# A decoder layer on one core: cross-attention's probabilities turned in two 64-row tiles, its values summed by 64 keys, register reads moved, all engines reordered

## The reference

```
scores = einsum('bhqd,bhkd->bhqk', qh, kh) * DH ** -0.5
scores = where((j <= i) & (j >= i - 32), scores, -1e30)
out = einsum('bhqk,bhkd->bhqd', softmax(scores), vh)  ->  out @ wo.T
```

## Time and profile before

| | |
|---|---|
| median of 3 runs | 791.24 us (790.92 to 792.99) |
| the profiled execution | 793.52 us |
| its span | 790.7 us, mean granted clock 0.987 |
| busy share of the span: PE, PEld | 96%, 80% |
| DVE, ACT, POOL | 68%, 68%, 68% |
| chain that ended last | PE 91%, DVE 3%, issue 2% |

### The profile page before, as it was taken

One profiled execution on the slowest core, in us unless ns is written; L12 is line 12 of the kernel. 1 busy time (PEld: TensorE's weight loads), 2 busy tenths in 40 slices (PEclk: granted clock), 3 DMA queues, 4 the chain that ended last, 5 costly groups with the idle time before them and its releaser, 6 DMA issues.

```text
span 790.7 us, 28613 instructions
## 1 busy us (share of the span) xinstructions
PE 759.4 (96%) x10349; PEld 631.8 (80%) x10349; DVE 536.6 (68%) x1350; ACT 539.2 (68%) x1900; POOL 535.4 (68%) x864
## 2 busy tenths in 40 slices
PE   7999999999999999999999999999899999999894
PEld 4778878888888888888888888888679778777563
DVE  3466767777777777777777777777866686665553
ACT  1367767777777777777777777777667667666352
POOL 3366777777777777777777777777565666576434
PEclk8999999999999999999999999999999999999998
DMA  6013212222222222222222222223043132133130
GB/s 232 12 56 124 80 61 82 88 91 93 92 93 73 73 73 73 72 73 73 73 73 73 73 73 72 73 73 128 9 129 125 48 101 72 40 104 123 55 101 12
DMA packets 56791, 64.06 MB, mean 81 GB/s; under 512 B 4014, under 2 KB 52916, under 8 KB 56656
## 3 DMA queue, kind: packets, MB, share of 16 engines
q1 hardware_dynamic: 52928, 54.06, 20.9%
q0 software_dynamic: 3008, 6.57, 2.4%
q10 hardware_dynamic: 720, 1.63, 0.5%
HBM read 17.80 MB, written 45.35 MB: 80 GB/s over the span
## 4 chain that ended last, share of the span: by engine, by line
PE 91%; DVE 3%; issue 2%; DMA 1%; ACT 1%; POOL 1%; SPq 0%; POOLq 0%; DVEq 0%; ACTq 0%
PE P L327 8%; PE P L272 8%; PE P L307 7%; PE P L292 7%; PE P L316 7%; PE P L338 7%; PE P L282 7%; PE P L397 5%; PE P L224 4%; PE P L207 4%; PE P L356 4%; PE P L239 4%; PE P L247 2%; PE P L364 2%; PE P L410 1%
## 5 line engine op out<-in xcount | busy, mean ns | idle before, releaser
L799 ACT ACTIVATE PX<-P,mx 128x128 f32<-128x128 f32 x512 | 182.1, 394 | 61.0 <-DVE mx L569 61.0
L966 POOL TENSOR_TENSOR PX<-PX,mx 128x512 f32<-128x512 f32 x128 | 133.0, 1041 | 62.0 <-DVE mx L574 62.0
L569 DVE TENSOR_REDUCE mx<-P 128x4 f32<-128x512 f32 x128 | 82.0, 679 | 119.3 <-PE P L307 119.3
L799 ACT ACTIVATION_READ_ACCUMULATOR PX<-P,mx 128x1 f32 x512 | 119.9, 234 | 0.0
L763 ACT ACTIVATE PS<-P 128x512 f32<-128x512 f32 x128 | 66.1, 602 | 32.0 <-PE P L228 32.0
L999 POOL DMA_INDIRECT out<-yst,xrow x46 | 46.0, 1000 | 54.6 <-DVE yst L673 42.5
L508 DVE TENSOR_REDUCE nmf<-P 128x4 f32<-128x512 f32 x128 | 79.5, 683 | 5.1 <-PE P L207 2.2
L961 POOL TENSOR_TENSOR rq<-rq,tq 128x1024 f32<-128x1024 f32 x32 | 75.7, 2365 | 8.8 <-DVE tq L533 7.8
L808 ACT ACTIVATE PT<-P 128x512 f32<-128x512 f32 x128 | 77.7, 607 | 3.5 <-PE P L316 0.8
L956 POOL TENSOR_TENSOR rk<-rk,tk 128x1024 f32<-128x1024 f32 x32 | 75.5, 2359 | 0.0
L272 PE MATMUL P<-wvT,cxT 128*128 128x512 f32 x128 | 70.4, 633 | 3.0 <-DVE tk L533 3.0
(11 more groups left out here) (144 smaller groups left out, 1757.4 us busy)
## 6 DMA issues: line engine op xcount, KB each, us to landing
z_xs<-c SPq DMA_DIRECT2D x34, 1088.0 KB, 5.3
xrow<-z_xs SPq DMA_DIRECT2D x46, 136.0 KB, 2.1
ew<-in_ew SPq DMA_DIRECT2D x9, 384.0 KB, 6.4
x<-in_x SPq DMA_DIRECT2D x32, 64.0 KB, 1.8
cxT<-in_ctxT SPq DMA_DIRECT2D x31, 64.0 KB, 1.7
out<-yst,xrow POOLq DMA_INDIRECT x46, 2.3
wk<-in_wk SPq DMA_DIRECT2D x1, 512.0 KB, 4.4
wvT<-in_wvT SPq DMA_DIRECT2D x1, 512.0 KB, 7.0
```

The lines of the kernel that those rows point to most:

```text
L569: dve.tensor_reduce(mx[b % 3][:, 0, r, :], v3(bank(f"ds{r}")), AX.X, ALU.max, negate=True).then_inc(S["v_dm"][r], 1)
L799: t = act.activation(PX[(4 * b + r) % 6][:, c, :], p[:, c * 128:c * 128 + 128], ACT.Exp, bias=m[:, 0, r, c:c + 1], scale=1.0, accum_out=m[ ...
L966: pool.tensor_tensor(X[:, :, :], X[:, :, :], mx[b % 3][:, 2, r, :].rearrange("p (h a) -> p h a", a=1).to_broadcast([128, 4, 128]), ALU.mul ...
```

## The change

1. `d_t` handles half k (8 heads) in one call. A transpose takes 64 query rows of PX instead of 128, so it has 64 columns of identity to stream and uses 64 of the array's rows; the two row halves u go to two PSUM banks. There are 32 transposes a batch for 16.
2. `PT` becomes 3 buffers of 8 heads for 6 of 4. `d_pt` still makes 4 copies of 512 elements a batch, now into columns 64u to 64u+64 of each head.
3. `d_pv` runs in tiles of 64 rows x 64 columns: `lo` multiplies keys 0 to 63 by queries 0 to 95 (96 columns), `hi` keys 64 to 127 by queries 64 to 127 (64 columns), into two banks. 32 matmuls a batch for 16.
4. ACT `d_ox` makes two copies (128 and 384 elements) for one of 512, and a new DVE `d_ox` adds `hi` to `lo` for queries 64 to 95 (128 elements); `d_wo` waits for DVE's.
5. The register read of tile j+1 stands behind `x_up(j)`'s matmul (`place`), no longer in `x_tr`.
6. The lists of all five engines, `BANK` and `WARM` are new. Cut short:

```diff
-            def d_t(b, r):
-                p = take(f"dt{r}", b, (S["s_pt"][r], b + 1))
-                pe.wait_ge(S["p_pn"][r], b + 1)
-                for c in range(4):
-                    t = pe.transpose(p[:, c * 128:c * 128 + 128], PX[(4 * b + r) % 6][:, c, :], ident[:, :])
-                t.then_inc(S["t_dt"][r], 1)
+            def d_t(b, k):
+                p = [take(f"dt{2 * k + u}", b, (S["s_pt"][2 * k + u], b + 1)) for u in range(2)]
+                for g in range(2):
+                    r = 2 * k + g
+                    pe.wait_ge(S["p_pn"][r], b + 1)
+                    for c in range(4):
+                        for u in range(2):
+                            t = pe.transpose(p[u][:, 256 * g + 64 * c:256 * g + 64 * c + 64],
+                                             PX[(4 * b + r) % 6][64 * u:64 * u + 64, c, :],
+                                             ident[64 * u:64 * u + 64, 64 * u:64 * u + 64])
+                t.then_inc(S["t_dt"][k], 1)
             def d_pv(b, k):
-                p = take(f"dpv{k}", b, (S["s_ox"][k], b + 1))
+                lo = take(f"lo{k}", b, (S["s_ox"][k], b + 1))
+                hi = take(f"hi{k}", b, (S["v_ox"][k], b + 1))
                 pe.wait_ge(S[f"s_v{k}"], b + 1)
-                for r in (2 * k, 2 * k + 1):
-                    pe.wait_ge(S["s_pt"][r], b + 1)
-                    for i in range(2):
-                        for u in range(2):
-                            q = 2 * (r % 2) + i
-                            t = pe.matmul(p[64 * u:64 * u + 64, 128 * q:128 * q + 128], V[b % 3][:, 4 * r + 2 * i + u, :],
-                                          PT[(4 * b + r) % 6][:, 2 * i + u, :], start=True, stop=True)
+                for u in range(2):
+                    pe.wait_ge(S["s_pt"][2 * k + u], b + 1)
+                for q in range(4):
+                    for u in range(2):
+                        pe.matmul(lo[64 * u:64 * u + 64, 96 * q:96 * q + 96], V[b % 3][0:64, 8 * k + 2 * q + u, :],
+                                  PT[(2 * b + k) % 3][0:64, 2 * q + u, 0:96], start=True, stop=True)
+                    for u in range(2):
+                        t = pe.matmul(hi[64 * u:64 * u + 64, 64 * q:64 * q + 64], V[b % 3][64:128, 8 * k + 2 * q + u, :],
+                                      PT[(2 * b + k) % 3][64:128, 2 * q + u, 64:128], start=True, stop=True)
                 t.then_inc(S["t_pv"][k], 1)
@@ x_up, after its matmul
+                if j + 1 < NT and j + 1 not in TILE0:
+                    place(j + 1)
@@ DVE
+            def d_ox(b, k):
+                o, hi = oX[2 * (b % 2) + k][:, :, 64:96], bank(f"hi{k}")[:, 0:256]
+                dve.wait_ge(S["s_ox"][k], b + 1)
+                dve.tensor_tensor(o, hi.rearrange("p (h q) -> p h q", h=4)[:, :, 0:32], o, ALU.add).then_inc(S["v_ox"][k], 1)
@@ ACT d_ox
-                act.activation(oX[2 * (b % 2) + k][:, :, :].rearrange("p h q -> p (h q)"), bank(f"dpv{k}"),
+                lo, hi = bank(f"lo{k}")[:, 0:384], bank(f"hi{k}")[:, 0:256]
+                act.activation(oX[2 * (b % 2) + k][:, :, 96:128], hi.rearrange("p (h q) -> p h q", h=4)[:, :, 32:64],
+                               ACT.Copy)
+                act.activation(oX[2 * (b % 2) + k][:, :, 0:96], lo.rearrange("p (h q) -> p h q", h=4),
                                ACT.Copy).then_inc(S["s_ox"][k], 1)
```

More of the change, by code:

```diff
@@ L415, in _ @@
             for s in range(PERIODS):
[L416 to L456, removed]
@@ L457, in _ @@
-                batch(b_ln, s - 5)
-                batch(d_t, s - 6, 1)
-                batch(d_t, s - 6, 2)
+                batch(b_s, s - 3)
+                tile(x_up, s - 31, 0)
+                tile(x_dn, s - 32, 1)
+                tile(x_hT, s - 32, 3)
+                batch(c_v, s - 3, 1)
+                batch(b_ln, s - 4)
+                tile(x_dn, s - 32, 2)
+                tile(x_tr, s - 31, 2)
+                batch(d_pv, s - 5, 0)
+                batch(r_q, s - 4, 0)
+                batch(e_tr, s - 6)
@@ new lines, in _ @@
+                batch(r_q, s - 4, 1)
+                batch(d_t, s - 5, 1)
+                batch(b_nm, s - 3)
+                tile(x_dn, s - 32, 3)
+                batch(f_pos, s - 7)
+                batch(f_up, s - 6)
+                batch(d_pv, s - 5, 1)
+                batch(b_st, s - 3)
+                batch(d_s, s - 4)
+                tile(x_hT, s - 31, 0)
+                tile(x_tr, s - 31, 3)
+                tile(x_up, s - 31, 1)
+                batch(b_pv, s - 3)
+                batch(d_wo, s - 5)
@@ new lines, in _ @@
+                batch(b_oT, s - 3)
+                tile(x_dn, s - 31, 0)
+                tile(x_up, s - 31, 2)
+                batch(r_k, s - 2, 0)
+                batch(a_qkv, s - 2)
+                batch(b_cn, s - 3)
+                batch(f_dn, s - 6)
+                tile(x_tr, s - 30, 0)
+                tile(x_hT, s - 31, 1)
+                batch(c_v, s - 2, 0)
+                batch(b_x1, s - 3)
+                batch(a_tr, s - 1)
+                tile(x_up, s - 31, 3)
+                tile(x_tr, s - 30, 1)
@@ L460, in _ @@
+                tile(x_hT, s - 31, 2)
+                batch(r_k, s - 2, 1)
+                batch(d_t, s - 4, 0)
             for j in range(TILE0[1], NT + 4):
@@ L676, in _ @@
             for s in range(PERIODS):
[L677 to L688, removed]
@@ new lines, in _ @@
+                batch(r_q1, s - 5)
+                batch(r_q3, s - 5)
+                batch(f_pos, s - 8)
+                tile(x_y, s - 33, 3)
+                batch(f_route, s - 7)
+                batch(f_gate, s - 7)
+                batch(d_ox, s - 6, 1)
+                batch(d_max, s - 5, 1)
+                batch(a_stats, s - 1)
+                batch(d_max, s - 5, 3)
+                batch(d_max, s - 5, 0)
+                batch(d_ri, s - 5, 1)
+                batch(d_max, s - 5, 2)
@@ L890, in _ @@
+                tile(x_xT, s - 32, 0)
+                tile(x_hT, s - 33, 1)
+                tile(x_th, s - 33, 3)
+                tile(x_hT, s - 33, 2)
+                tile(x_xT, s - 32, 1)
+                batch(c_v, s - 4, 0)
+                batch(a_norm, s - 2)
+                batch(d_pt, s - 6, 1)
+                batch(d_pt, s - 6, 0)
+                batch(b_ln, s - 5)
+                tile(x_th, s - 32, 0)
+                batch(e_norm, s - 7)
                 tile(x_hT, s - 33, 3)
+                batch(b_cT, s - 5)
```

160 lines of the change are left out of this document (75 added, 85 removed).

## The result

| | median | range (runs) |
|---|---|---|
| before, beside it | 792.12 us | 790.92 to 800.3 (4) |
| changed | **824.36 us** | 820.7 to 830.44 (4) |
| ratio | 1.0392 | 95% interval 1.0293 to 1.0491 |

The change costs 32 us; I had forecast 18 us less than before and a range up to 789. The profiled execution took 820.7 us.

The account below looks back on a forecast made before the run. PE was taken to bound the kernel, only its own time counting. 793.5 - 21.8 (turns) + 3.5 (`b_pv` wait) - 3.5 (reads) + 2.8 (end) + 1.0 (shape change in tile turns) = 775.5 us profiled, median 773, range 763 to 789.

Parts of the forecast that it names:

- `d_t`, `d_pv`: PE's transposes and value matmuls: smaller tiles run side by side, -0.80 and -0.43 us a batch.
- rivals B and C: B: weight loads bound `d_pv`'s four-tile groups, 787 us, chance 0.07. C: its row halves don't overlap, 801 us, 0.09.
- Changes of shape: PE's switches of tile shape: 11 a turn for 7, at 0.14 us each, +0.55 us a turn (0.4 to 0.75).
- The new wait at `b_pv`: PE waits in front of `b_pv` for ACT's exponentials: +0.13 us (0 to 0.25) in 27 turns, +3.5 us.
- rival A: The new order's waits take half the gain, two places missing by 0.15 us: 9.6 us back, 783 us, chance 0.20.
- the sum of a turn itself: A turn, one batch on PE: -0.80 - 0.43 + 0.55 = -0.68 us, from 20.30 to 19.6 to 19.75; 32 turns, -21.8 us.
- In such a stretch only PE's own time counts: From 200 to 240 us PE is busy all 40.00 us; the other engines have a quarter to spare.
- a floor of 25 ns: The skill's minimum between PE matmul starts, by which `d_pv` gains 0.14 instead of 0.43 us; set aside for L228's 14 ns.
- `hi1`'s bank: `d_s` takes over this bank after DVE's add: 1.98 us needed, PE there after 2.03; no cost, or 0.1 to 0.3 a turn.
- Register reads: PE's reads moved from in front of `x_tr` to behind `x_up`, mostly covered there: -3.5 us (-5 to -1).
- The end: From batch 31's `f_pos` to chunk 1's first tile: 3.4 us of PE work moves ahead, scatter 0.6 sooner, +2.8 us.

Follow-up runs that it names:

- order alone: Computation of the kernel before, in the changed kernel's new order, with the register reads moved: 824.7 us (ratio 1.0384), on another chip 855.4 us (1.0771).
- `d_pv` undone: Changed kernel with the old `d_pv`, ACT's one copy of 512 elements and no DVE add: 848.7 us, ratio 1.0697 to the kernel before.

## Why the prediction was wrong, by its own steps

- **`d_t`, `d_pv`: right.** Forecast 0.58 to 0.63 (0.48 and the shape) and 0.75 to 0.85 us a block; measured 0.64 and 0.81. Pairs and fours do run side by side; rivals B and C didn't happen.
- **Changes of shape: too small.** 11 x 0.14 less the old 7 came to +0.55. The rows behind the new blocks say more: L292 1.09 for 0.89, L216 0.16 for 0.06, L348 1.98 for 1.89, L239 1.08 for 1.01, 0.46 us. My sum was -0.68 in all with some -0.81 in the four blocks, which left 0.13 for this.
- **The new wait at `b_pv`: right place, half its size.** ACT's four exponentials took 297.57 to 299.63, and `b_pv` started 0.37 us later, where I had 0.1. From `b_st`'s end to `b_pv` it is 2.47 us, for 2.17 of `d_s` before: +0.30, not +0.13. The row of after calls this "issue"; ACT's end at 299.63 and the order alone's row speak for ACT. Together with the point above a turn is 20.2 and not 19.7: 32 x 0.5 = 16 us. The wait's part of that, 0.17 us a turn or 5 us, is rival A, which I gave 9.6 us.
- **The failed step is the sum of a turn itself, which knew columns, shapes and data and no instructions.** "In such a stretch only PE's own time counts" was read from a list with slack in its instruction supply. 22.6 us of the turns' excess, and a part of the last turns', are fetches. I had set 14 ns a record from L228 against a floor of 25 ns and taken it as proof that starts are free; 16 records in a row tell nothing of a block's end. The Trainium skill ("Advanced Engine Details and Errata", Engine Queue Depths) gives a TensorE queue of 64; by that, an estimate, 64 instructions cover 0.95 us of a 2.2 us fetch at this stretch's 67 per us, and 1.07 at the old stretch's 60. That is too small a difference to tell nine stalls from none in `d_s`, so the depth isn't what decides here; no run shows it. What the traces do show is how late the packet starts.
- **`hi1`'s bank: the margin was right, the turn of `tile_table` was not looked at.** "Each costs nothing by my count" holds in the ordinary turns; behind `tile_table` it is 7.6 us, of which 6.8 to 7.0 stay when the add is gone (order alone, `d_pv` undone): the new order's wait for `gu`'s bank, which I hadn't looked at. Moving the table won 1.5 to 3 us, so most of it was hidden in what came after.
- **Register reads: right and under-sized**, -6.5 and -5.9 us for -3.5 (-5 to -1).
- **The end: wrong sign, from a misread row.** From the last `f_pos` to the last matmul it took 41.8 us for 42.8, where I had +2.8. The 752.57 of the earlier trace rows is chunk 1's second tile; behind chunk 0's 31 tiles its first is the 32nd record of L392, in front of which PE had hardly stood (the first row below). So PE's own work set the 14.2 us from `f_pos` (737.09) to there, and not the chain outside it. With about half of that work gone from behind `f_pos`, the way is 11.6 us (766.11 to 777.74), and now PE does stand, 3.3 us, for the load. The scatter left 6.1 us behind `f_pos`, 7.0 before.

```profile
751.25 0.33 PE L392 MATMUL P<-c,xrow 128*128 128x128 f32 x1 [0.19 <-issue]
```

```profile
766.11 0.17 PE L389 MATMUL P<-acc,ones 128*128 128x8 bf16 x1
...
777.74 0.45 PE L399 MATMUL P<-c,xrow 128*128 128x128 f32 x1 [3.34 <-DMA xrow<-z_xs]
```

```profile
772.19 0.98 POOL L1018 DMA_INDIRECT z_xs<-er,pos  x1 [0.28 <-POOL er L1012]
```

The sum of the miss is 45 us by the profiled executions (820.7 for 775.5). 34 of them lie in turns 3 to 26: 23 in fetches, and 24 x 0.47 = 11 in the turn itself (20.22 for 19.75: shapes, ACT). The other 11 lie ahead of them, in the last five turns and behind those. There the turn of `tile_table` took 29.6 us for 22.7 and the next one 25.6 for 28.9, one more stall at L307 took 3.6, the reads won 3 more than forecast and the end 4 more; these overlap and weren't worked apart.

## What to carry to other kernels

Count an engine's instructions per microsecond beside its columns: where a change trades few large matmuls for many small ones, or packs small ones together, look in "issue" for idle time without a partner and at the instruction queue's packets. An order is a resource of its own: try new order and new computation apart, as here the order cost 31.6 us (with 6 us of the register reads' gain inside it), more than the computation won (25 us, 32 x 0.79 by quiet turns). Once a stretch lives at that limit, its time depends on where it is run and on how many instructions stand ahead of it, so time it on more than one chip.

## What the runs showed of the hardware that I had not expected

- A crossing from one 256-instruction block to the next can cost 1.0 to 3.6 us of idle time: PE never crossed sooner than 2.2 us after the packet's start. In the stretch of some 67 PE instructions per us the place fell into `d_s` 18 times and stalled it 9 times; with 60 per us, in the kernel before, 16 times and never, though two crossings beside its `d_s` cost 1.1 and 1.6 us. 68 us lie between two kernels that differ in 54 pairs of met waits at the start.
- Chips, or the hours at which they ran, differ in such a stretch: 827 and 867 us for one program; from its first record to its last L307 takes 1.76 or 2.17 us in quiet turns, and 1.8 to 2.1 or 5.1 to 7.4 in the last four; the kernel before differed by 1 to 2 us. What in the chip it is stays open.
- On the second of these two chips the last part also shows a lower granted clock: 0.91 from 560 to 850 us with PE busy 87 to 90% of it, 0.93 to 0.95 on the first with 91 to 92%, each a mean of stretches at 2.4 and at 1.2 GHz; the kernel before has 1.00 and 0.97 from 560 to 780 us, busy 94 to 97%. What the clock alone costs there wasn't taken apart. The rows, second chip, then first (from:to, length, PE and PEld, DVE, ACT, POOL, granted clock):

```profile
720.00:850.00 130.00, 112.91 (x1033) 80.63 (x1031) 66.19 (x203) 62.13 (x216) 64.88 (x85) 0.91 0.22 65
```

```profile
706.00:816.00 110.00, 99.94 (x1015) 72.78 (x1012) 65.18 (x201) 61.38 (x213) 63.76 (x83) 0.95 0.25 76
```
